# Cross-attention and quantised feed-forward on one core: the transposing transfer of normalised x is issued as two transfers, one per half word

## What is computed

```python
x = x + xattn(layernorm(x), ctx, ctx, Wq, Wk, Wv, Wo)   # 16 heads of 32, rope on q and k, softmax over 120 keys
x = x + ffn(layernorm(x), w_gate, w_up, w_down)         # 512 -> 1536 -> 512

def ffn(x, ...):                       # 4-bit weights in blocks of 32, activations rounded to 16 bits
    x = act_qdq(x)                     # one scale for the whole tensor: max|x| / 32767
    up, gate = act_qdq(x @ deq(w_up).T), act_qdq(x @ deq(w_gate).T)
    gate = act_qdq(gate * fixed_qdq_u16(sigmoid(gate)))
    return act_qdq(gate * up) @ deq(w_down).T
```

## Time and profile before

| | us |
|---|---|
| median of the 3 runs | 2328.13 |
| the profiled execution | 2326.45 |
| span of its instructions | 2324.6 |
| TensorE busy in the span | 2203.7 (95%) |
| VectorE busy | 1685.1 (72%) |
| ScalarE busy | 1329.8 (57%) |
| GpSimd busy | 701.5 (30%) |
| 16 DMA engines, share of hardware-issued packets | 66.9% |

### The profile page before, as it was taken

How to read it: one execution, slowest core, us unless ns; L and a number is a source line. 1 busy time by engine, 2 the same in 40 slices (tenths; PEclk the granted TensorE clock), 3 DMA queues, 4 the chain that set the end, 5 groups by cost and what they waited for, 6 DMA issues and landing times. The chain is left out here.

```text
span 2324.6 us, 31131 instructions
## 1 busy us (share of the span) xinstructions
PE 2203.7 (95%) x12037; PEld 971.1 (42%) x12037; DVE 1685.1 (72%) x1690; ACT 1329.8 (57%) x1299; POOL 701.5 (30%) x655
## 2 busy tenths in 40 slices
PE   5898999999998899999999999999998799999999
PEld 3443333333333444444444444444443344444444
DVE  7656788889876766445543598888888887778773
ACT  3345566666654233222322787877877777777772
POOL 3444566666664301000100264444444000000000
PEclk8899999999999999999999999999999899999999
DMA  6333667777777577888875898877776555655552
GB/s 189 97 103 101 168 173 189 170 193 173 193 169 182 154 232 244 265 245 254 255 229 180 286 336 306 303 283 290 292 281 260 188 223 221 235 220 204 209 217 91
DMA packets 286711, 500.14 MB, mean 215 GB/s; under 512 B 187500, under 2 KB 189804, under 8 KB 249692
## 3 DMA queue, kind: packets, MB, share of 16 engines
q1 hardware_dynamic: 286556, 498.09, 66.9%
HBM read 247.75 MB, written 186.58 MB: 187 GB/s over the span
## 5 line engine op out<-in xcount | busy, mean ns | idle before, releaser
L1694 PE MATMUL banks<-XB,W 128*128 128x512 f16 x2304 | 498.9, 380 | 2.3 <-ACT XB L1720 2.3
L1694 PE MATMUL banks<-XB,WT 128*128 128x512 f16 x2304 | 497.4, 379 | 0.0
L2160 PE MATMUL banks<-W,OH 128*128 128x512 f16 x2256 | 488.8, 380 | 2.5 <-DVE OH L2262 2.5
L1714 ACT ACTIVATE OB<-banks,uns 128x512 f32<-128x512 f32 x384 | 255.7, 684 | 391.2 <-PE banks L1694 388.6
L1694 PEld LDWEIGHTS banks<-XB,W 128*128 128x128 f16 x2304 | 225.7, 98 | 275.1 <-issue 3.4
L1694 PEld LDWEIGHTS banks<-XB,WT 128*128 128x128 f16 x2304 | 225.4, 98 | 271.8
L2160 PEld LDWEIGHTS banks<-W,OH 128*128 128x128 f16 x2256 | 221.1, 98 | 270.2 <-DVE OH L2262 3.0
L1981 POOL TENSOR_TENSOR PR<-GS,OB 128x2048 f32<-128x2048 f32 x46 | 220.6, 4795 | 257.5 <-ACT OB L1714 247.6
L1803 DVE TENSOR_REDUCE amx<-OB 128x1 f32<-128x2048 f32 x48 | 109.7, 2285 | 238.2 <-ACT OB L1714 238.2
L748 PE MATMUL banks<-XC,AH 128*128 128x512 f16 x768 | 179.3, 385 | 3.2 <-POOL AH L1506 1.6
L689 PE MATMUL banks<-XD,WQ 128*128 128x512 f16 x768 | 179.2, 383 | 2.5 <-DVE WQ L1127 1.2
(11 more groups left out here) (272 smaller groups left out, 2904.5 us busy)
## 6 DMA issues: line engine op xcount, KB each, us to landing
g_s<-OB SPq DMA_DIRECT2D x48, 1024.0 KB, 6.1
GL<-g_s SPq DMA_DIRECT2D x48, 1024.0 KB, 7.5
up_s<-OB SPq DMA_DIRECT2D x48, 1024.0 KB, 4.9
XA<-up_s SPq DMA_DIRECT2D x32, 1024.0 KB, 9.3
gq_s<-GQ SPq DMA_DIRECT2D x48, 512.0 KB, 4.8
XD<-gq_s SPq DMA_DIRECT2D x48, 512.0 KB, 6.7
XA<-in_x SPq DMA_DIRECT2D x16, 1024.0 KB, 6.7
QW<-QE SPq DMA_DIRECT2D x128, 128.0 KB, 2.9
```

The costliest lines, as they stand in the source:

```text
L1694: t = e.matmul(pk[:].rearrange("p (j t) -> p j t", j=4), WT[w][:, ot, wa, kk, :], XB[i % 2][:, xa, :, kk, :], start=(kk == 0 and wa == 0 a ...
L1714: e.activation(OB[n % 3][:, r, :], bank[(k + 4) % 8][:], ACT.Copy, scale=uns[:, 12 * w + ot:12 * w + ot + 1]).then_inc(s_ev, 1)
L2160: t = e.matmul(pk[:].rearrange("p (r n) -> p r n", r=4), OH[i % 2][:, a, ot, j * 128:(j + 1) * 128], WD[:, :, c, wa, o4, :], start=(ot == ...
```

## The change

The turn of x is issued as two transfers of half the size. The first, of the high halves, stands where the one transfer stood, and waits for the high halves alone. The second, of the low halves, waits for the low halves. Up to step 13 (batches 1 to 4) it follows the first at once; from step 17 on (batches 5 to 15) it is issued one step later, behind that step's exchange of pairs and ahead of the load of x. Every waiter on the turn counts two transfers in place of one.

```diff
-        def sp_x_turn(e, b):
-
-            e.wait_ge(s_xlo, 2 * b + 2)
+        def sp_x_turn(e, b, a):
+
+            e.wait_ge((s_xhi, s_xlo)[a], 2 * b + 2)
             if b == 1:
                 e.wait_ge(s_wlo, 2)
             if b >= 2:
                 e.wait_ge(s_q, 4 * (b - 2) + 4)
-            e.dma_start_transpose(XD[b % 2][:].rearrange("p a j (k t) -> p (a j k) t", t=128),
-                                  ST.rearrange("p a j d -> p (a j d)")).then_inc(s_xt, 16)
+            e.dma_start_transpose(XD[b % 2][:, a, :, :].rearrange("p j (k t) -> p (j k) t", t=128),
+                                  ST[:, a, :, :].rearrange("p j d -> p (j d)")).then_inc(s_xt, 16)
...
                 for nb in [1] if s == 2 else x_at(s, 2):
-                    sp_x_turn(e, nb)
+                    sp_x_turn(e, nb, 0)
+                    if s < 16:
+                        sp_x_turn(e, nb, 1)
+                for nb in x_at(s - 1, 2) if s > 16 else []:
+                    sp_x_turn(e, nb, 1)
                 if c == 2 and 2 <= b + 2 < B:
                     sp_x_load(e, b + 2)
...
-                            e.wait_ge(s_xt, 16 * (B - 1))
+                            e.wait_ge(s_xt, 32 * (B - 1))
...
             if c == 0 and b:
-                e.wait_ge(s_xt, 16 * b)
+                e.wait_ge(s_xt, 32 * b)
...
             if b >= 2:
-                e.wait_ge(s_xt, 16 * (b - 1))
+                e.wait_ge(s_xt, 32 * (b - 1))
```

## The result

Over 6 executions each, the kernel before has a median of 2328.72 us (2325.9 to 2331.02) and the changed one 2317.47 us (2313.8 to 2320.1): a ratio of **0.9949** (95% interval 0.9937 to 0.9961), 11.25 us faster. The forecast was 2317.6. On another chip the same kernel gave 2319.12 beside 2327.74, a ratio of 0.9954 (0.9937 to 0.9972). The profiled execution took 2318.47 us, 7.98 less than the profiled one of before. The traces can account for those 8 us alone; the further 3.3 lie in where the two profiled executions stand to their medians. (A ratio is estimated with its interval over all executions, so it can differ by up to 0.001 from the ratio of the two medians beside it.)

A forecast was written before the change was run, and what follows sets the result against it. TensorE, busy 95% of the span, was taken as the bound, so only its idle time could be won. -10.5 + 2 - 2 = -10.5 us from 2326.45 gives 2316.0; medians lie 1.7 above, so 2317.6 us, range 2304 to 2332.

The forecast's parts named there:

- the tail: From step 57 on: one more issue, idle room on SyncE; nothing, with 1 us either way.
- c = 3: The 11 such steps in 17 to 60: exchange no longer held by the turn's issue, excess gone, -10.5 us (0 to -10.5).
- Within 1 us of the eviction: Sign of success: exchange of steps 18, 22, ... issued that soon, in place of 3 to 5 us.
- half of a held one (7.13 / 2) 3.6: High half's issue on SyncE in c = 1 steps: proportional to size, so 3.6 us when held, freeing SyncE at 421.9.
- The free price: Issue of a half turn where nothing holds it: 2.45 us, taken as proportional to size.
- the second hold: Rival, chance 0.10: low turn held again, load of x 1.5 us later, c = 0 steps cost 21.6 us; 2337 in all.
- c = 0: The 11 such steps: TensorE arrives 0.96 us earlier, load of x only 0.6; +2 us (bounds -6.2 and +8).
- the prediction's own signs of being wrong: Among them: load of x later against c = 0 scores, and those steps passing 10 us in most batches.
- Batches 1 to 4: Both transfers together, the first issued while the low halves are made: -2 us (bounds 0 and -5).
- Idle room on SyncE: Reason given for the tail from step 57 on costing nothing despite one more issue.
- c = 1 and 2: Steps 17 to 60 of these kinds: no term in the sum; their lengthening would show the forecast wrong.

The follow-up runs named there:

- e2_whole_later: Against the kernel before: one unsplit turn, issued a step later behind the exchange from step 17 on, batches 1 to 4 as before; 2325.6 us, ratio 0.9973.
- e1_split_in_place: Against the kernel before: turn split in two halves, both left at the old place in every batch; 2336.47 us, ratio 1.0026.
- e7_high_ahead: Against the changed kernel: high half's turn ahead of its step's two broadcasts instead of behind them, from step 17 on; 2316.86 us, ratio 0.995 to the kernel before.
- e4_load_first: Against the changed kernel: load of x issued ahead of the low half's turn instead of behind it; 2324.35 us, ratio 0.9975 to the kernel before.
- e6_deviation_first: Against the changed kernel: GpSimd's inverse deviation ahead of the sine instead of behind it, late steps only; 2322.53 us, ratio 0.9971 to the kernel before.
- e9_recip_after: Against the changed kernel: reciprocals' way out issued behind the exchange of c = 0 steps instead of ahead; 2323.03 us, ratio 0.9963 to the kernel before.
- e3_split_late_only: Against the changed kernel: split and move kept for batches 5 to 15 alone, batches 1 to 4 with one transfer; 2323.41 us, ratio 0.997 to the kernel before.
- e10_high_ahead_gate: Against the changed kernel: high turn ahead of the broadcasts, and gate weight turns issued in pairs in other steps; 2313.36 us, ratio 0.9929 to the kernel before.

## Why the prediction was right, and where it was not

The forecast of 2317.6 was met to 0.13 us by the median and to 2.5 by the profiled execution (2316.0 forecast, 2318.47), partly by luck: its terms were -10.5, +2 and -2, with the tail and c = 1 and 2 at nothing, and four of the five measured ones differ from them by 2 us and more, with opposite signs.

**c = 3: -10.5 forecast, -9.65 measured; right, and for the reason given.** The turn's issue held the exchange, and the exchange the scores. e2_whole_later, which does nothing but take the turn out of the way, goes to 95.69; e1_split_in_place, which does nothing but split, goes to 114.66. "Within 1 us of the eviction" holds in e2_whole_later and, but for one step, in e7_high_ahead; in the changed kernel the exchange is 1.79 us late on the mean and up to 2.9. Against the 4.11 of before that is 2.3 earlier, just about the 2.04 that were needed. Not all of the gain is idle time: 2.0 of the 9.65 us are TensorE's busy time, most of it in step 35, which had 10.39 us busy at a granted clock of 0.86 and has 8.77 at 1.00 now. One sum in this part is off without harm: behind an addition at 430.2, MX comes at 431.8, by the 1.55 us between the two in the earlier trace rows, and not at 430.9; it still ends ahead of 435.34.

**The step that failed: the high half's issue, "half of a held one (7.13 / 2) 3.6".** It measured 4.6 to 6.5. The hold is not proportional to the turn's size. What fits all runs, and is inferred from them, is the time that the transfers ahead of it still need, plus a small part of its own: ahead of the broadcasts the half took 1.74 to 2.03 us in most batches (e7_high_ahead), behind two broadcasts about 5, behind the load up to 7.98. The free price was too high as well, 2.45 against 1.74. The DMA side agrees. Stretches of the kernel after, in the first of which the high half is held (it is issued at 406.44), and in the third the low half (issued at 414.45); share and GB/s stand last:

```profile
409.00:411.00 2.00, 2.00 (x25) 0.96 (x18) 2.00 (x2) 1.67 (x4) 1.92 (x3) 1.00 0.26 85
412.00:416.00 4.00, 4.00 (x35) 1.32 (x34) 3.76 (x9) 1.44 (x3) 4.00 (x5) 1.00 1.04 274
416.00:418.00 2.00, 2.00 (x11) 0.78 (x8) 1.40 (x3) 2.00 (x2) 1.24 (x2) 1.00 1.20 106
418.00:426.00 8.00, 7.69 (x65) 2.81 (x64) 5.63 (x6) 3.86 (x7) 4.92 (x4) 1.00 1.00 301
```

At 409 to 411 the engines run at a share of 0.26 and 85 GB/s, much as during the hold of before. At 416 to 418 the share is 1.20 with 106 GB/s: packets that stand and wait. This is **the second hold**, the rival with a chance of 0.10, in part: over the 11 late batches the high halves average 5.6 us and the low ones 3.2, together 8.8, against 6.8 for the whole before. Its mechanism was there, its verdict was not.

**c = 0: +2 forecast, +5.22 measured.** I had SyncE free at 421.9 and the load 1.2 us earlier than before; it came 1.06 later. The scores' side came 0.89 us earlier per step, as forecast (0.96), so the load is late by 1.95 against it, and c = 0 pays 0.52: the chain had some 1.4 us of slack, where the rival reckoned with 0.5. That is why the second hold did not cost 21.6 us. Two of the prediction's own signs of being wrong are met here: the load is later against the scores, and six of the 11 steps with c = 0 pass 10 us. The run e7_high_ahead, in which the load goes out 0.80 us earlier, gives back 0.91 per batch; e4_load_first, e6_deviation_first and e9_recip_after show that the order of the load, the deviation or the exchange of c = 0 alone does not do it. The load as the first link is the reading that fits best; how the cost divides among load, exchange and shift is not shown.

**Batches 1 to 4: -2 forecast (0 to -5), -5.48 measured.** The reason was right, the size was not. I had booked 2 us for the four, from the 1.5 us that SyncE is free sooner in batch 1 and at best as much again for batches 3 and 4 together. Batch 1 shortens step 3 by 1.6, of which steps 4 and 5 give back 1.0; batch 4 alone brings 5.0. SyncE's queue with the turn of batch 4 (step 13), and the eviction of step 14, before:

```profile
228.38 0.69 ACT L994 ACTIVATE QE<-banks,qsc 128x512 f32<-128x512 f32 x1 [0.60 <-PE banks L712]
230.29 4.89 SPq L433 DMA_TRANSPOSE XD<-XA  x1
235.28 0.55 SPq L398 DMA_DIRECT2D QW<-QE  x1
```

and after:

```profile
221.93 8.34 SPq L433 DMA_TRANSPOSE XD<-XA  x2
226.95 0.68 ACT L998 ACTIVATE QE<-banks,qsc 128x512 f32<-128x512 f32 x1
230.35 0.55 SPq L398 DMA_DIRECT2D QW<-QE  x1
```

Before, the issue waited for the low halves, until after the eviction; now the high half starts while they are made, and the exchange is 3.4 us behind the eviction's start in place of 6.9. The two steps from the eviction of step 14 on take 15.8 in place of 20.8: 5.0, most of the 5.48.

**The tail: 0 forecast with 1 either way, +4.27 measured.** This was the worst term. SyncE's queue before, in steps 60 and 61:

```profile
674.20 2.88 SPq L488 DMA_TRANSPOSE W<-wt_s  x1
...
679.60 0.53 SPq L398 DMA_DIRECT2D QW<-QE  x1
```

and after, with the sine behind it:

```profile
664.60 3.04 SPq L488 DMA_TRANSPOSE W<-wt_s  x1
...
669.82 0.53 SPq L398 DMA_DIRECT2D QW<-QE  x1
```

```profile
680.00 1.26 POOL L1480 TENSOR_TENSOR QW<-QW,sq 128x512 f32<-128x512 f32 x1 [6.85 <-DMA QW<-QE]
```

Step 61's queries leave the bank at 678.88 before and at 665.67 after. So the turn of a weight was issued 4.7 us ahead of them and is now 1.1 ahead, and the exchange goes out 3.5 us late in place of 0. The sine starts 10.2 us behind the issue (10.3 before), and step 61 is 3.3 longer. But the late issue is not all: in the second profile of the changed kernel the exchange goes out only 1.3 us late, the sine starts 12.3 behind it, and step 61 is as long (17.35). What sets the landing stays open. The rest is the clock: in step 62 the granted clock is 0.70 of full speed (before 0.82), behind 5.9 idle us of TensorE in step 61 (before 2.6), and TensorE is busy for 9.51 us in place of 8.58. The loss comes with the move: e2_whole_later has 26.39, e3_split_late_only 26.91, but e1_split_in_place 23.15. With the weight's turns elsewhere most of it is gone (24.28, against 23.36 before), and in e10_high_ahead_gate all of it (20.99 at a clock of 1.00). "Idle room on SyncE" was said of a queue in which a transposing issue stands in each step, of 2.9 and 4.0 us in steps 60 and 61.

**c = 1 and c = 2: 0 forecast, -2.35 measured** (-3.17 in the other execution). No experiment isolates this; it stays open.

**The price of an issue.** The split adds 15 issues. A half that little is ahead of holds SyncE for 1.74 us, against 4.87 for the least of the whole in e2_whole_later, and the two halves of batches 1 to 3 together for 4.4 to 4.7, against 4.9 for the whole before: no fixed cost shows that is paid again. The fixed cost of about 2.0 us per DMA that the Trainium skill's page "DMA: Bandwidth & Descriptors" gives in "Anatomy of one DMA", for DMAs that GpSimd issues, would be 30 us for 15 more, as an estimate from that page; no run here shows it on the issuing side. In its "Rules for kernel authors" the Trainium skill's page asks to merge many small transfers, and calls those under 64 KB mostly overhead; the halves have 512 KB. In steps 17 to 60 of e1_split_in_place, which take 432.41 us against 420.81, two transfers in place of one did cost time; in batches 1 to 4, where the first half can start before the second is made, they did not.

## What to carry to other kernels

Ask of a transposing transfer not how large it is but what is still draining ahead of it, and put neither it behind broadcasts or a large load nor a small, urgent transfer behind it. A move that frees one step can make the later transfers of the same queue late against engines that now come sooner, so look at each one that follows, in the steps at the end of the loop too. In this kernel splitting paid where the first half could start before the second existed; elsewhere it was the move, not the split, that brought the gain.

## What the hardware showed that I had not expected

- The issue of one and the same half turn (128 x 4 x 512 float16, 512 KB) took from 1.74 to 7.98 us by what stood ahead of it, and SyncE was held for that time. The plain issues in the queues above (L398, L424) took 0.5 to 0.6, the load of 1 MB among them; the longest L398 of the steps from 17 on took 1.5.
- Behind broadcasts two halves side by side hold longer than the whole (7.3 to 9.5 us in the 11 late batches of e1_split_in_place, against 5.2 to 7.9 for one before); in batches 1 to 3, with no broadcasts ahead, they do not (4.5 to 4.8 against 4.9).
- While a transposing transfer waits for its turn, the engines' share can pass 1 at 106 GB/s: a share near 1 is not a sign of full use without the GB/s beside it.
